# The load of the next x moved ahead of a group's writes, its statistics moved from steps 11 to 15 to steps 7 to 9

## The reference

```python
xn = layer_norm(x, norm_w, norm_b)
q = (xn @ q_w + q_b).reshape(Bx, Tx, H, -1)
k = (xn @ k_w + k_b).reshape(Bx, Tx, H, -1)
att = jnp.einsum('bnhl,bmhl->bnmh', q, k)
att = att + (1.0 - mask) * -1000000.0
att = jax.nn.softmax(att, axis=2)
v = ((xn @ v_w + v_b) * src_mask[:, :, None]).reshape(Bx, Tx, H, -1)
y = jnp.einsum('bnmh,bmhl->bnhl', att, v).reshape(Bx, Tx, Dx)
e = jax.nn.silu(emb) @ emb_w + emb_b
scale, shift = jnp.split(e[:, None, :], 2, axis=2)
h = layer_norm(y, sb_norm_w, sb_norm_b) * (1.0 + scale) + shift
h = jax.nn.silu(h) @ out_w + out_b
return x + h
```

## Time and profile before

| | |
|---|---|
| median of 3 runs | 521.43 us (519.89 to 522.01) |
| the profiled execution | 522.72 us, span 521.0 us |
| TensorE busy | 503.0 us, 97% |
| VectorE busy | 408.0 us, 78% |
| ScalarE busy | 356.2 us, 68% |
| GpSimd busy | 225.3 us, 43% |
| mean granted TensorE clock | 0.997 |
| HBM traffic | 109 GB/s over the span |

### The profile page before, as it was taken

The page is one execution under the profiler, slowest core; times in us unless marked ns, Lnnn a source line. Parts: engine busy times, 40 slices in busy tenths (PEclk is TensorE's granted clock), DMA queues, the critical chain, the costliest instruction groups (busy, mean ns, idle before and its releaser), DMA issues.

```text
span 521.0 us, 10061 instructions
## 1 busy us (share of the span) xinstructions
PE 503.0 (97%) x2831; PEld 189.4 (36%) x2834; DVE 408.0 (78%) x657; ACT 356.2 (68%) x647; POOL 225.3 (43%) x270
## 2 busy tenths in 40 slices
PE   8898999999999999999999999999999999998787
PEld 3422333343333333333333434343433333332225
DVE  6696778888798978888788878888788877888714
ACT  2305777667876778677877777677777777666783
POOL 4365324436335643536335543545345444334101
PEclk9989999999999999999999999999999999999999
DMA  5335444234434443235434444235433342234002
GB/s 155 111 116 163 124 124 134 79 93 125 129 89 123 132 140 113 79 101 153 127 99 122 108 132 125 79 107 151 134 102 115 104 133 83 82 113 128 0 2 81
DMA packets 54586, 57.42 MB, mean 110 GB/s; under 512 B 12424, under 2 KB 41736, under 8 KB 54560
## 3 DMA queue, kind: packets, MB, share of 16 engines
q1 hardware_dynamic: 51808, 54.74, 36.0%
q10 hardware_dynamic: 2752, 2.37, 1.6%
HBM read 35.82 MB, written 21.00 MB: 109 GB/s over the span
## 4 chain that ended last, share of the span: by engine, by line
PE 85%; DVE 4%; issue 3%; POOL 3%; ACT 3%; DMA 1%; SPq 0%; POOLq 0%; ACTq 0%; DVEq 0%
PE pv_ps L577 24%; PE st_ps L561 22%; PE mx_ps L525 12%; PE job_ps L640 9%; PE job_ps L649 5%; PE job_ps L661 3%; DVE negmax L952 2%; PE mx_ps L686 2%; ACT probs L745 2%; PE mx_ps L538 2%; PE mx_ps L620 1%; PE mx_ps L694 1%; PE pv_ps L461 1%; DMA k_rows<-qk_dram 1%; DVE x_stats L956 0%
## 5 line engine op out<-in xcount | busy, mean ns | idle before, releaser
L952 DVE TENSOR_REDUCE negmax<-mx_ps 128x2 f32<-128x1024 f32 x256 | 304.7, 1219 | 83.2 <-PE mx_ps L525 82.9
L745 ACT ACTIVATE probs<-st_ps 128x512 f32<-128x512 f32 x502 | 272.3, 595 | 116.5 <-PE st_ps L561 115.8
L561 PE MATMUL st_ps<-q_rows,k_rows 115*128 115x512 bf16 x502 | 155.1, 383 | 3.2 <-ACT probs L745 2.8
L577 PE MATMUL pv_ps<-probs,v_rows 128*32 128x512 f32 x1024 | 136.4, 605 | 0.6 <-ACT probs L745 0.6
L1225 POOL TENSOR_TENSOR qk_parts<-qk_rest,qk_parts 128x512 bf16<-128x512 f32 x31 | 36.0, 1161 | 133.0 <-DVE qk_parts L1026 133.0
L525 PE MATMUL mx_ps<-k_rows,q_rows 51*128 51x512 bf16 x512 | 79.4, 383 | 2.1 <-DMA k_rows<-qk_dram 2.1
L561 PEld LDWEIGHTS st_ps<-q_rows,k_rows 115*128 115x128 bf16 x502 | 39.1, 97 | 105.0 <-ACT probs L745 71.7
L1210 POOL TENSOR_TENSOR qk_parts<-qk_full,zero 128x512 bf16<-128x512 f32 x29 | 30.2, 1042 | 77.1 <-ACT qk_full L767 77.1
L640 PE MATMUL job_ps<-x_norm_t,w_qk 128*128 128x512 f32 x116 | 59.5, 593 | 0.0
L525 PEld LDWEIGHTS mx_ps<-k_rows,q_rows 51*128 51x128 bf16 x512 | 15.8, 94 | 111.0 <-DVE negmax L952 53.0
L1216 POOL TENSOR_TENSOR qk_rest<-qk_full,qk_parts 128x512 f32<-128x512 f32 x31 | 35.9, 1158 | 4.3 <-ACT qk_parts L759 2.0
(11 more groups left out here) (126 smaller groups left out, 390.3 us busy)
## 6 DMA issues: line engine op xcount, KB each, us to landing
qk_dram<-qk_parts SPq DMA_DIRECT2D x128, 128.0 KB
q_rows<-qk_dram SPq DMA_DIRECT2D x124, 96.0 KB, 2.6
k_rows<-qk_dram SPq DMA_DIRECT2D x124, 96.0 KB, 2.6
x_in<-in_x SPq DMA_DIRECT2D x16, 256.0 KB, 3.0
x_res<-in_x SPq DMA_DIRECT2D x7, 512.0 KB, 4.4
out<-out_sb SPq DMA_DIRECT2D x14, 256.0 KB, 2.6
k_rows<-mask_dram SPq DMA_DIRECT2D x64, 6.0 KB
w_e<-in_L_cond_emb_w ACTq DMA_DIRECT2D x4, 256.0 KB, 2.9
```

What stands on the lines that cost most here:

```text
L561: pe.matmul(st_bank(b, t, h), k_rows[0:ROWS_ALL, g, h, c * P:(c + 1) * P], q_rows[0:ROWS_ALL, g, h, :], start=True, stop=True).then_inc(st ...
L577: mm = pe.matmul(pv_ps[VW * h:VW * (h + 1), :], v_rows[:, c, g * GH + h, :], probs[:, t % P_SLOTS, h, :], start=(c == 0), stop=(c == CH - ...
L745: act.activation(probs[:, t % P_SLOTS, h, :], st_bank(b, t, h), ACT.Exp).then_inc(exp_done, 1)
L952: dve.tensor_reduce(by_pair[:, :, j, c], mx_ps[j][:, :, :], AXIS_X, ALU.max, negate=True).then_inc(max_done, 1)
```

## The change

SP issues the two DMAs of the next x ahead of `spread(b, 0, 1)`, right behind the load of x_res. On VectorE the four statistics of x go from (11, 0), (11, 2), (12, 2), (13, 1) to (7, 0), (7, 2), (8, 0), (8, 2), and the moments from (15, 0) to (9, 1). No instruction is added or removed.

```diff
-X_STAT = {(11, 0): (0,), (11, 2): (1,), (12, 2): (2,), (13, 1): (3,), (15, 0): (4,)}
+X_STAT = {(7, 0): (0,), (7, 2): (1,), (8, 0): (2,), (8, 2): (3,), (9, 1): (4,)}
...
                     sp.dma_start(x_res[:, :, :], batch_of(x_dram, b - 1)).then_inc(res_loaded, 16)
-                spread(b, 0, 1)
                 if exists(b + 2) and not (isinstance(b, int) and b == -1):
 
                     wait_apart(sp, maskp_ready, x_norm_ready, CH * (b + 2))
                     load_x(b + 2)
+                spread(b, 0, 1)
                 spread(b, 1, 1)
                 spread(b, 2, 1)
```

## The result

The changed kernel takes 523.13 us (median of 17 runs, 521.46 to 525.79), the kernel before 521.43 us (17 runs). The ratio is 1.0035, with a 95% interval of 1.0023 to 1.0048: 1.8 us slower by the ratio, 1.7 by the two medians, somewhere from 1.2 to 2.5 by the interval, and within the 0.5% that the forecast calls no change. The forecast was +1.3 us. The profiled execution has a span of 521.1 us and a mean granted clock of 0.997, TensorE is busy for 96%.

What follows compares the result with a forecast made beforehand. TensorE, busy for 97%, was taken to set the time, with VectorE touching it only at the turns of the maxima. The terms -2.0 + 3.3 + 0 = +1.3 us put the median of 521.43 at 522.7, range 520.7 to 524.3.

Steps and rivals of the forecast that it cites:

- Part 1: Statistics leave steps 11 to 15: the one at (13, 1) gives back 0.33 us in 6 bodies, 2.0 us gained.
- rule that what is put elsewhere fits into idle time: VectorE work costs in full only between the two reduces of the step ahead of a turn; elsewhere it is free.
- Part 2: Statistics enter steps 7 to 8 free; moments at (9, 1) delay step 10's turn by 0.55 us, 3.3 us in all.
- Part 3: Load of x ahead of group 0's writes: lands at about 244.7, 1 us before TensorE would stall; cost 0.
- The cost term of 0: Moving the load of x ahead of group 0's writes on SP's queue was to add no time.
- The prediction's own sign of being wrong: VectorE waiting for x in step 7 was among the signs that would show the forecast wrong; no size given.
- The late x: Rival at (7, 0): x lands late, stalling 0.95 us in each of 5 bodies, 527.5 us; chance 0.07.
- The moments at no cost: Rival at step 10: the moments cost nothing and only the gain of 2.0 stays, 519.4 us; chance 0.07.
- The durations added, 1.0: Rival at (9, 1): the moments cost their summed durations, 1.0 us each, +4.0, 525.4 us; chance 0.03.
- The change without effect: Rival at the turns: stall and moments both stay as they are, 521.4 us; chance 0.06.
- Pool's chain: At the body's end, Pool reaches the moments late, so having them earlier gains nothing.

Runs made afterwards that it cites:

- the six kernels: The changed kernel and five experiments on it, all with a statistic at (7, 0) and the load of x behind x_res; ratios 0.9977 to 1.0062 to the kernel before.
- five relatives: Changed kernel with moments at (11, 0): 0.9987, (8, 1): 0.9977, or (9, 2): 1.0018; or one more statistic at (9, 1): 1.0062, or (8, 1): 1.0033.

## Why the prediction was right, point by point

**Part 1** was right in its sum. The stall of step 14 is one statistic between two reduces. It is gone in the changed kernel, in all six bodies (270.19 is 0.58 after its matmuls), and in the kernel before with that one statistic moved. The other statistics of steps 11 to 13 gave nothing back. The prediction's rule that what is put elsewhere fits into idle time is too wide: the moments at (9, 2), just behind the two reduces, cost 0.36 a body at the pairs of step 10, and one statistic at (14, 2) cost 0.14 in step 0 of the next body. It held for the four statistics of the change, as each reduce behind them still had idle time ahead of it.

**Part 2** was right. Predicted 0.55 at the turn of step 10, from a row of the same seven instructions; measured 0.56 in six bodies. Predicted growth from turn to turn 0.2, measured 0.23. The sum of parts 1 and 2 was +1.3; the loop distance grew by 1.46. With 0.56 and 0.32 to 0.34, it is 6 x 0.23 = 1.4, and the other 0.07 is what the load alone adds to the loop. That the place decides and not the work was shown twice: the moments cost nothing at (8, 1) and at (11, 0), and a statistic more costs 0.33 at (9, 1) and nothing at (8, 1).

**Part 3** was right in its deadline and too sure of its margin. The deadline (a statistic at (7, 0) is free only if x is there, and beyond 0.12 more TensorE stalls at the transposes of h) is what the late bodies show. The landing was put at 244.7, 6.2 us after the issue of x_res and with a margin of 1 us, from the medians of two rows. It was 5.2 us after it in the body shown, and from 5.2 to 7.6 in the 30 bodies of the six kernels, in 9 of which VectorE waited. The 1.8 for x behind x_res was near (1.4 in most bodies); what was mis-sized is the 4.4 for x_res itself, a median that stands for landings of up to 6.2. The cost term of 0 should have been about 0.3 us an execution by the six profiled ones. With it the sum would be 1.46 + 0.3 = 1.8, but 1.46 alone also lies within the interval of 1.2 to 2.5, and the changed kernel's one profiled execution has no late body: that late bodies filled the difference is argued from its five relatives. The prediction's own sign of being wrong, VectorE waiting for x in step 7, is absent from this profile and present in four of the five relatives, so that it is absent here is in part luck; four late bodies in one execution cost 0.9 us, so with a few the time would have stayed within the stated range. The late x and its cure, the other order of the two loads, are shown.

**The rivals.** The moments at no cost: refuted by the 0.56 idle before the turn. The late x: the mechanism exists, with its place, and was thought unlikely at 0.07; it occurs in some bodies of most executions, but at 0 to 0.6 us for a late body and not 0.95 in each of five. The rival let x land 3.0 to 4.4 us after x_res; it landed 1.4 to 2.8 after it. It doesn't make the kernel slower by over 0.5%. The durations added, 1.0: refuted, the start times gave 0.56. The passage of the Trainium skill that the prediction names (VectorE: DVE Perf Modes, "The DRAIN you can't avoid") goes on to say that a next operation that isn't held back starts earlier. The traces agree with this second half: the additional statistic lasts 0.42 and costs 0.33. The change without effect: refuted, the old stall went and the new one came.

**Pool's chain** gave no gain, as said: from the turn of step 14 to that of step 6 in the next body, a stretch with both transposes of x, it is 29.49 us in the changed kernel and 29.48 before. The kernel with only the table of before changed keeps its moments at (15, 0) and is among the fastest.

## What to carry to other kernels

Where one engine is full and others only meet it at a few handshakes, look for the handshakes and the deadline of each: the same small operation costs its start-to-start time in one place of an order, part of it in the next place and nothing in a third, so find the idle time behind every place before choosing it, and the next deadline behind that. A transfer moved to just behind a larger one is to be judged by the latest landing of both and not by the medians, for the wait hits in some rounds only and one profile can miss it.

## What the runs showed that was not expected

The landing of the same 256 KB loads, placed behind 512 KB, varied from 4.1 to 6.4 us within the loop of one execution, and there were from none to four late bodies in five between executions of nearly the same kernel; ahead of the 512 KB the latest took 3.9.

In the course of 10 us of idle time TensorE's granted clock fell to half, and stayed there for the first 4.1 us of work, which added 2.1 us to a stall of 10. None of the stalls of 0.3 to 0.9 us did that; in all the other kernels' loops the granted clock stayed at full speed.

The start-up ahead of the loop differs by up to 2.7 us between executions (the first turn of body 0 lies between 46.3 and 49.0 in the 14 profiled ones), which is more than the change is worth: spans of single executions don't tell such changes apart, the distance between two marks in the loop does.
